# Thirty statistics exchanges issued by SyncE between its loads instead of by GpSimd

## What is computed

```python
def _layer_norm(x, gamma, beta, eps=1e-05):
    mean = jnp.mean(x, axis=(-2, -1), keepdims=True)
    var = jnp.mean(jnp.square(x - mean), axis=(-2, -1), keepdims=True)
    return (x - mean) * jax.lax.rsqrt(var + eps) * gamma + beta
...
out = jax.nn.silu(scale * _layer_norm(x, gamma, beta) + shift)
out = out @ W_in + b_in
out = jax.nn.silu(scale * _layer_norm(out, gamma, beta) + shift)
out = out @ W_out + b_out
x = out + x
...
h = jax.nn.gelu(jnp.einsum('bsh,bhi->bsi', x, Wi[expert]) + bi, approximate=False)
o = jnp.einsum('bsi,bih->bsh', h, Wo[expert]) + bo
r = o + x
# then a norm of each row of r, eps 1e-12, with the expert's gamma and beta
```

## Time and profile before

| | us |
|---|---|
| median of 3 runs | 1776.24 (1775.8 to 1776.51) |
| the profiled execution, own time | 1775.97 |
| its span in the profile | 1774.3 |
| PE busy | 1764.1 (99%) |
| DVE busy | 1286.5 (73%) |
| ACT busy | 977.4 (55%) |
| POOL busy | 108.2 (6%) |
| queue q1, share of 16 DMA engines | 29.6% |
| queue q0 | 2.0% |

### The profile page before, as it was taken

How to read it: one execution, slowest core, us unless ns; L and a number is a source line. 1 busy time by engine, 2 the same in 40 slices (tenths; PEclk the granted TensorE clock), 3 DMA queues, 4 the chain that set the end, 5 groups by cost and what they waited for, 6 DMA issues and landing times.

```text
span 1774.3 us, 22297 instructions
## 1 busy us (share of the span) xinstructions
PE 1764.1 (99%) x7941; PEld 1455.3 (82%) x7941; DVE 1286.5 (73%) x2145; ACT 977.4 (55%) x1551; POOL 108.2 (6%) x198
## 2 busy tenths in 40 slices
PE   9999999999999999999999999999999999999998
PEld 6888888888888888888888888888888888888886
DVE  6876777767777777767777677677777777767576
ACT  4756554565545656456564555655556554565442
POOL 1100000000000000000000000000000000000000
PEclk9999999999999999999999999999999999999999
DMA  7332232323333233231333313333143232322321
GB/s 292 98 111 75 99 110 85 142 77 100 109 120 110 74 122 110 98 111 71 123 110 101 117 63 122 117 115 110 58 140 107 99 110 89 139 76 79 127 96 59
DMA packets 45665, 189.35 MB, mean 107 GB/s; under 512 B 7091, under 2 KB 7347, under 8 KB 29044
## 3 DMA queue, kind: packets, MB, share of 16 engines
q1 hardware_dynamic: 43156, 183.96, 29.6%
q0 software_dynamic: 2400, 3.97, 2.0%
HBM read 171.10 MB, written 16.81 MB: 106 GB/s over the span
## 4 chain that ended last, share of the span: by engine, by line
PE 99%; DVE 1%; DMA 0%; SPq 0%; issue 0%; ACT 0%; DVEq 0%
PE out_acc L531 39%; PE hid_ps L531 39%; PE blk_ps L531 18%; DMA stage<-in_W 0%; PE out_acc L561 0%; SPq L350 0%; PE out_acc L549 0%; PE out_acc L465 0%; DVE x L930 0%; PE out_acc L572 0%; PE hid_ps L549 0%; PE out_acc L573 0%; PE out_acc L576 0%; DVE x_lo L825 0%; PE blk_ps L549 0%; PE hid_ps L456 0%
## 5 line engine op out<-in xcount | busy, mean ns | idle before, releaser
L531 PE MATMUL hid_ps<-x_hi,wi_hi 128*128 128x512 f32 x1024 | 398.6, 389 | 0.1
L531 PE MATMUL hid_ps<-x_hi,wi_lo 128*128 128x512 f32 x1024 | 398.4, 389 | 0.0
L531 PE MATMUL hid_ps<-x_lo,wi_hi 128*128 128x512 f32 x1024 | 398.4, 389 | 0.0
L531 PE MATMUL out_acc<-wo_hi,g_hi 128*128 128x512 f32 x1012 | 393.7, 389 | 0.0
L531 PE MATMUL out_acc<-wo_lo,g_hi 128*128 128x512 f32 x1012 | 393.7, 389 | 0.0
L531 PE MATMUL out_acc<-wo_hi,g_lo 128*128 128x512 f32 x1012 | 393.7, 389 | 0.0
L719 ACT ACTIVATE g_sb<-hid_ps,bi_sb 128x512 f32<-128x512 f32 x256 | 176.0, 687 | 311.2 <-PE hid_ps L531 310.9
L825 DVE TENSOR_TENSOR g_lo<-g_sb,g_hi 128x512 fp32r<-128x512 f32 x253 | 173.3, 685 | 182.7 <-ACT g_hi L723 181.0
L679 ACT ACTIVATE wo_hi<-stage 128x512 fp32r<-128x512 f32 x253 | 160.2, 633 | 172.2 <-PE out_acc L531 172.1
L531 PEld LDWEIGHTS hid_ps<-x_hi,wi_hi 128*128 128x128 f32 x1024 | 192.1, 188 | 40.4 <-DVE x_lo L825 0.8
L531 PEld LDWEIGHTS hid_ps<-x_lo,wi_hi 128*128 128x128 f32 x1024 | 192.3, 188 | 39.9
(11 more groups left out here) (166 smaller groups left out, 1680.6 us busy)
## 6 DMA issues: line engine op xcount, KB each, us to landing
stage<-in_expert_w SPq DMA_DIRECT2D x128, 1024.0 KB, 4.9
x<-in_xT SPq DMA_DIRECT2D x15, 1024.0 KB, 6.9
out_y<-r_sb SPq DMA_DIRECT2D x15, 1024.0 KB, 5.3
rows<-in_expert_rows SPq DMA_DIRECT2D x16, 512.0 KB, 6.8
mv_all<-mv_dram POOLq DMA_DIRECT2D x30, 128.0 KB, 4.2
stage<-in_cond_w SPq DMA_DIRECT2D x4, 512.0 KB, 10.0
affine_sb<-in_affine SPq DMA_DIRECT2D x3, 512.0 KB, 10.1
x<-in_xT SPq DMA_DIRECT2D x4, 256.0 KB, 3.8
```

The source lines that it names most:

```text
L531: last = pe.matmul(dst, w[wp], xs[xp], start=start and i == 0, stop=stop and i == 2)
```

## The change

`spread` moves from GpSimd's list to SyncE's. Two numbers for each sample say after which pair load it stands: after pairs 3 and 6 for sample 1 (in b = 0), after pairs 1 and 5 of sample b for sample b+1. The semaphores and both DMAs of it stay what they are. GpSimd keeps `norm_rstd`.

```diff
+SPREAD_AFTER = ((3, 6), (1, 5))
...
+            def spread(b, which):
+
+                turn = turn_of(b, which) - 2
+                sp.wait_ge(s_mv, turn_of(b, which) + 1)
+                sp.dma_start(mv_dram[turn].rearrange("(p a) -> p a", a=2), mv[:, which, :]) \
+                  .then_inc(st_mv, 16)
+                sp.wait_ge(st_mv, 16 * (turn + 1))
+                sp.dma_start(mv_all[:, which, :, :].rearrange("p a n -> p (a n)"),
+                             mv_dram[turn:turn + 1, :].to_broadcast([P, 2 * P])) \
+                  .then_inc(ld_mv, 16)
...
                     if j == 4 and 1 <= b and b + 2 < B:
                         load_x(b + 2)
+                    if b + 1 < B and j in SPREAD_AFTER[min(b, 1)]:
+                        spread(b + 1, SPREAD_AFTER[min(b, 1)].index(j))
...
-            def norm_stats(b, which):
-                spread(b, which)
-                norm_rstd(b, which)
...
-            norm_stats(1, 0)
+            norm_rstd(1, 0)
...
                 for b, _ in block_a_due(k, X_STATS):
-                    norm_stats(b, 0)
+                    norm_rstd(b, 0)
                 for b, m in block_a_due(k, W_IN):
                     if m == DC - 1:
-                        norm_stats(b, 1)
+                        norm_rstd(b, 1)
```

More of the change, by code:

```diff
@@ L1170, in _ @@
         def _(pool):
[L1171 to L1180, removed]
             def power(b, which, ve):
```

## The result

The changed kernel takes 1834.89 us in the median of 5 runs (1829.03 to 1837.15), the kernel before 1776.07 on the same chip: a ratio of 1.0325, 95% interval 1.0314 to 1.0337, 58.8 us slower. Forecast were 1822 us and a range of 1786 to 1843. The profiled execution of it is the shortest of the five, 1829.03, with a span of 1827.3 us, 53.0 us over that of before.

A forecast was written before the change was run, and what follows sets the result against it. TensorE, without a gap for 97% of the span, was taken as the bound. Late exchanges would make PE wait 3.5 us thirteen times, 46 us; 1775.97 + 46 gave 1822 us, range 1786 to 1843.

The forecast's parts named there:

- The bound: TensorE busy without a gap from 48.7 us to 1763 us; the change matters only by opening gaps on PE.
- signs against it: Much shorter waits, PE gaps at another product such as an up waiting for wi_lo, or a clock row below 1.00.
- T: Start of DVE's totals once mv_all has landed; predicted 644.6 in the period studied, between 641.8 and 646.0.
- The slack and the formula: Chain from DVE's totals to PE's first W_OUT product: PE waits T - 641.04 us per period, nothing when T is earlier.
- The write: SyncE's write of mv behind input load and pair 5: lands at 641.6, low end 639.8.
- The read: SyncE's 128 KB read of mv_all after the write lands: 2.8 us, ends 1.8 and 4.2.
- Pair 6: Load queued on SyncE behind the read, out at about 642.2, there by 647, used after 656: no cost.
- The first exchanges: Part of the other seventeen exchanges: mv_all lands by 581.7, before totals at 582.2, so no cost.
- The rival that the exchange isn't held up: SyncE's write gets past the pair or through gaps in the loads; T stays below 641.04: 1776 us, chance 9%.
- GpSimd's 60 DMAs are worth nothing: Removing sixty issues of some 0.6 us from GpSimd gains nothing, as its next work waits for DVE's totals.
- The clock: Rival: clock drops to 1.2 GHz after each PE gap, 2.7 us more per period, 13 times: 1857 us, chance 8%.

The follow-up runs named there:

- held pair 6 back: Changed kernel with SyncE issuing pair 6 only after the read of mv_all has landed, in the 13 periods: 1806.49 us, ratio 1.0176 to the kernel before.
- behind the input alone: All exchanges on SyncE, the 13 between input load and pair 5 instead of behind both as in the changed kernel: 1788.22 us, ratio 1.0063 to the kernel before.
- with the gap filled: Changed kernel plus 12 useless matmuls before the first W_OUT product in samples 2 to 14: 1819.33 us, ratio 1.024 to the kernel before.

## Why the prediction was right, and what in it was not

*The bound.* Right: no wait of another engine counts until it opens a gap on PE. The places are right in the main. 35.1 of PE's 41.0 us of waiting are at the 13 W_OUT products named; the other 5.9 us are at an `up`, 12 times, where the prediction had "none elsewhere". Its list of signs against it names two things that did come, gaps at an `up` waiting for wi_lo and a clock row below 1.00. The first doesn't upset the sum, since a later T brings as much more waiting whichever of the two gaps takes it, as the periods show. The second is a cost that the sum left out.

*The slack and the formula.* Right, and the part that carried the rest. It was worked out from one late landing of the trace before and two idle times of DVE. The four kernels with T below 11.17 have no gap, and for T from 11.6 to 17.9 the periods without a fall of the clock lie on it within 0.12 us. The changed kernel has 13 x 3.75 = 49 us by it against 46 predicted.

*The write.* Mechanism right, size wrong by 2.4 us. Said was that its bytes move when the pair's are through, and that it lands 2.3 us later, at 641.6, 11.7 us after the input load's issue. It lands at 651.30 + 8.35 = 659.65, 9.3 after it, below even the low end of 639.8. Bytes stop moving at about 657.8:

```profile
657.60:657.90 0.30, 0.30 (x3) 0.25 (x2) 0.00 (x0) 0.00 (x0) 0.00 (x0) 1.00 0.07 1
657.90:659.60 1.70, 1.70 (x9) 1.43 (x8) 0.00 (x0) 1.11 (x2) 0.00 (x0) 1.00 0.00 0
```

From there to the landing are 1.8 us, where I had taken 2.3: half a microsecond of the error. The other 1.9 us are the loads, which I had too long. I took pair 5's 9.2 us over from the trace before, where GpSimd's read of mv_all was issued together with pair 5. Without it the input lands in 5.3 us instead of 6.9 and the pair in 7.3 instead of 9.2. It is the read and not its queue: with the 13 exchanges on SyncE ahead of the input load, the read running beside the loads again, they take 7.4 and 9.3 in the median. The change took away the very DMA that had slowed the loads which it now stood behind.

*The read.* Mis-sized the other way, 5.7 us here (5.6 in the median) and not 2.8, which is outside the ends of 1.8 and 4.2 too. My nearest row, a 256 KB load into an empty queue, was the wrong neighbour: in the 17 exchanges with no input load ahead the read takes 4.1 us, about as long as the same read by the software queue, whose 4.2 I had in the earlier trace rows and used as the upper end only. The experiment that held pair 6 back shows another 1.5 us to be the load behind it. Pair 6 was in the text, as harmless because it lands in time; that it slows what stands ahead of it was not thought of. The errors of the two terms, -2.4 and +2.9 us, nearly cancelled in T (644.6 predicted, 644.95 in the same place of the period), and 1822 owes some of its nearness to that. This is luck: each of the two terms lies outside the ends that I gave it.

*The first exchanges.* Right, they cost nothing.

*The rival that the exchange isn't held up.* It falls: the write from SyncE lands in 8.4 us in the 13 and in 3.7 in the other 17, and the kernel is slower.

*GpSimd's 60 DMAs are worth nothing.* Wrong by 2 us. The end of the program waited for GpSimd's DRAIN, which is longer by them; no row of mine looked behind the last matmul.

*The clock.* I gave it 8% as a case of its own, 2.7 us in each period. It came true in a milder form together with the forecast: in the profiled run it fell in four of the periods and brought the twelve 6.7 us above the formula. For this run the sum closes: 49 + 6.7 - 2 = 53.7, and its span is 53.0 us longer than before. The median run is another 5.9 us longer. It has no trace, and its granted clock, 0.994 against 0.995, accounts for some 2 us of that as an estimate (0.001 of the span of 1830); the rest stays open. The 8% was for a fall after every gap; that some gaps would be followed by one, together with the forecast, was in none of the cases.

## What to carry to other kernels

A small DMA on which a chain depends belongs ahead of the large loads in its queue; on a queue of its own it was in time too, though there it was also issued before them. What stands directly behind it matters as well, and of two dependent DMAs the first is the one to keep free. When an engine is full without a gap, find from the latest harmless event of the trace how late each input may come, and price a change by that threshold: here it gave single periods within 0.12 us. When pricing a DMA behind others, take the others' times without the traffic that the change removes.

## What the runs showed of the hardware that was not expected

- A read of 128 KB broadcast from one row of 1 KB took about 4 us on either kind of queue in the 17 exchanges with no input load ahead (medians 4.1 from SyncE in the changed kernel, 4.0 from GpSimd in the kernel before, 3.8 where GpSimd issues only these 17), and the loads of 1 MB beside it landed later: the input in 7.2 us instead of 5.3, pair 5 in 9.2 instead of 7.3 (medians of the 13, before and changed).
- GpSimd's closing DRAIN lasted 0.65 us plus 0.082 us for each DMA that it had issued in the whole program, in traces with 0, 13, 26, 34 and 60 of them.
- The granted clock fell to half at some of PE's gaps and not at others of the same length, for 3.4 or 6.8 us at a time: in four of 13 periods of the changed kernel (gaps of 2.7 us), and in the kernel with pair 6 held back at gaps of 2.21 and 2.14 us, with no other gap in the period. At no gap of the kernel behind the input alone, up to 1.2 us long, did it fall.
- A fall of 3.4 us cost 1.3 to 1.6 us of the period, and nothing that can be measured where PE's next wait came soon after it. The changed kernel's runs lie 8 us apart and have a granted clock of 0.992 to 0.995; with the gap filled they lie 2 us apart at 0.999 to 1.000. This points to the clock for the spread, but the clock figures by themselves don't add up to all 8 us.
